# Edge rows in pairs of buffers, most of them summed by GpSimd, and a weight ring of three half chunks, in a one-core graph, attention and MLP layer

## The reference

```
xn    = layernorm(x)
e_f   = relu([xn[src], xn[dst]] @ W_class + b_class)      # one row per edge
logit = e_f @ W_a + b_a
alpha = softmax of logit over the edges with one dst
z     = segment_sum(alpha * xn[src], dst)
g     = relu([xn, z] @ W_hn or W_on + b)                   # 128 h nodes, 384 o nodes
x1    = x + g + linear_attention(xn)
out   = x1 + mlp(layernorm(x1))
```

## Time and profile before

| | |
|---|---|
| median of 3 runs | 787.0 us (785.25 to 787.54) |
| profiled execution, its own time | 785.15 us |
| its span (first to last instruction) | 783.4 us |
| mean granted TensorE clock | 0.923 |
| PE busy | 660.7 us (84%) |
| DVE busy | 505.2 us (64%) |
| ACT busy | 209.5 us (27%) |
| POOL busy | 259.7 us (33%) |
| moved by DMA | 163.40 MB |

### The profile page before, as it was taken

The page is one execution under the profiler, slowest core; times in us unless marked ns, Lnnn a source line. Parts: engine busy times, 40 slices in busy tenths (PEclk is TensorE's granted clock), DMA queues, the critical chain, the costliest instruction groups (busy, mean ns, idle before and its releaser), DMA issues. The chain is left out here.

```text
span 783.4 us, 8227 instructions
## 1 busy us (share of the span) xinstructions
PE 660.7 (84%) x2739; PEld 467.8 (60%) x2741; DVE 505.2 (64%) x1084; ACT 209.5 (27%) x266; POOL 259.7 (33%) x191
## 2 busy tenths in 40 slices
PE   4999999999847997798999699999955676798952
PEld 3778887788735775575778456677710011586621
DVE  8968813635645556365764597865568896327996
ACT  4333322220332354041614425152220100311001
POOL 3000306655654206247475555401223000002340
PEclk9999999999988999798999999999995779899985
DMA  9753449999999768969999999945360023140201
GB/s 347 257 203 135 141 184 298 296 323 320 323 303 317 269 200 226 306 200 312 306 287 296 317 318 236 303 151 189 108 242 0 0 80 135 54 140 5 108 27 80
DMA packets 41721, 163.40 MB, mean 209 GB/s; under 512 B 5168, under 2 KB 5552, under 8 KB 34512
## 3 DMA queue, kind: packets, MB, share of 16 engines
q0 software_dynamic: 20160, 73.41, 36.1%
q1 hardware_dynamic: 20800, 88.88, 30.1%
q10 hardware_dynamic: 720, 0.59, 0.2%
HBM read 146.08 MB, written 16.78 MB: 208 GB/s over the span
## 5 line engine op out<-in xcount | busy, mean ns | idle before, releaser
L1384 PE MATMUL bank_low<-w_hi,xT_hi 128*128 128x512 f32 x496 | 201.7, 407 | 8.2 <-DVE w_lo L861 3.2
L1385 PE MATMUL bank_low<-w_lo,xT_hi 128*128 128x512 f32 x496 | 196.4, 396 | 0.0
L1386 PE MATMUL bank_low<-w_hi,xT_lo 128*128 128x512 f32 x496 | 196.2, 396 | 0.0
L560 POOL DMA_INDIRECT gathered_rows<-edge_tables,dst_row x68 | 115.8, 1703 | 76.8 <-DMA gathered_rows<-edge_tables,src_row 65.5
L1029 DVE SCALAR_TENSOR_TENSOR gathered_rows<-gathered_rows,wa_bc 128x1024 f32<-128x1024 f32 x68 | 83.0, 1221 | 83.1 <-DMA gathered_rows<-edge_tables,dst_row 83.1
L560 POOL DMA_INDIRECT gathered_rows<-edge_tables,src_row x68 | 87.0, 1279 | 127.2 <-DVE gathered_rows L1029 91.8
L861 DVE TENSOR_TENSOR w_lo<-w_raw,w_hi 128x2048 fp32r<-128x2048 f32 x48 | 107.9, 2288 | 31.2 <-ACT w_hi L633 30.9
L1384 PEld LDWEIGHTS bank_low<-w_hi,xT_hi 128*128 128x128 f32 x496 | 95.3, 192 | 38.0 <-issue 12.3
L1386 PEld LDWEIGHTS bank_low<-w_hi,xT_lo 128*128 128x128 f32 x496 | 95.0, 191 | 20.6
L1385 PEld LDWEIGHTS bank_low<-w_lo,xT_hi 128*128 128x128 f32 x496 | 95.2, 192 | 18.7
L633 ACT ACTIVATE w_hi<-w_raw 128x2048 fp32r<-128x2048 f32 x50 | 92.8, 1902 | 8.3 <-DMA w_raw<-in_wt 8.3
(11 more groups left out here) (269 smaller groups left out, 951.7 us busy)
## 6 DMA issues: line engine op xcount, KB each, us to landing
w_raw<-in_wt SPq DMA_DIRECT2D x54, 1024.0 KB, 8.2
edge_tables<-stage SPq DMA_DIRECT2D x32, 256.0 KB, 7.1
x_in<-in_x SPq DMA_DIRECT2D x4, 512.0 KB, 9.1
xn_scratch<-xn SPq DMA_DIRECT2D x4, 512.0 KB, 4.6
node_top<-stage SPq DMA_DIRECT2D x8, 256.0 KB, 7.7
x_part<-in_x SPq DMA_DIRECT2D x8, 256.0 KB, 5.5
mix_out<-stage SPq DMA_DIRECT2D x8, 256.0 KB, 2.0
xn_raw<-xn_scratch SPq DMA_DIRECT2D x4, 512.0 KB, 5.8
```

What stands on the lines that cost most here:

```text
L560: pool.indirect_dma_start(rows_sum[:, s, :], None, table_d[0:rows, :], bass.IndirectOffsetOnAxis(ap=index[:, t:t + 1].bitcast(U32), axis=0 ...
L1384: pe.matmul(dest, lh, rh, start=start and i == 0, stop=False)
L1385: pe.matmul(dest, lh, rl, start=False, stop=False)
L1386: last = pe.matmul(dest, ll, rh, start=False, stop=last_one)
```

## The change

- **Buffers.** `SLOTS` goes from six single rows to five pairs: `rows[:, s, 0]` for src and `rows[:, s, 1]` for dst. `LAG` goes from 2 to 3 tiles.
- **Who sums.** Tiles with t % 3 == 2 (23 of 68) keep the DMA that adds. The other 45 gather both rows plainly, one after the other, and POOL sums them with a `tensor_tensor` of 128 x 1024 three tiles later.
- **Dots.** DVE takes single tiles (`edge_tile`), each with its mask, then the maximum of the tile before (`catch_up`), then its own dot. The table `TILES` gives for each chunk the tiles behind each of two points: after the low half 1 of chunk c, and after the low half 0 of chunk c + 1. Dots now go on up to PR0, and all 36 early lookups stand in PR1.
- **Weight ring.** The high and low parts lie in a ring of three half chunks (`w_half`) and not in two whole slots. PE goes through a chunk by halves: first k 0 to 3 of all row tiles, then k 4 to 7. High half 1 of chunk c + 1 can be made once the first halves of chunk c are multiplied (`first_halves`). SP loads half 1 of chunk c + 2 after the stores of chunk c.
- **Around the attention.** DVE's sums for K and Q follow all edge tiles of their chunk; `attend` and `invert_den` have new places; the products kv, den8 and attend on PE are placed by half.

```
-PAIRS = {4: 2, 5: 3, 6: 2, 7: 3, HHT0: 1, HHT1: 1, K0: 3, V0: 3, HN1: 1, K1: 3, V1: 3, Q0: 2, Q1: 3, ON0: 3, ON1: 1}
-MAXIMA = {PR0: (0, 18), PR1: (18, 36)}
+RING = 3
+TILES = {4: (0, 1), 5: (2, 3), 6: (2, 3), 7: (2, 3), HHT0: (1, 1), HHB0: (1, 1), HHT1: (1, 1), HHB1: (1, 1), K0: (3, 2), HN0: (0, 1),
+         V0: (3, 2), HN1: (0, 1), K1: (3, 2), V1: (3, 2), Q0: (3, 2), Q1: (2, 2), ON0: (2, 2), ON1: (2, 2), PR0: (3, 2)}
+MAXIMA = {PR1: (0, 36)}
-SLOTS = 6
+SLOTS = 5
+LAG = 3
+DMA_ADDS = [t for t in range(T_GATHERED) if t % 3 == 2]
+POOL_ADDS = [t for t in range(T_GATHERED) if t % 3 < 2]
...
+ATTEND = {(Q1, 1, 0): [(0, 0), (0, 1)], (Q1, 1, 1): [(0, 2), (0, 3)], (ON0, 1, 0): [(1, 0), (1, 1)], (ON0, 1, 2): [(1, 2), (1, 3)]}
+DEN8 = {(Q1, 0, 2): 0, (ON0, 0, 1): 1}
+KV_AT = {(HN1, 0, 0): 0, (Q0, 0, 0): 1}
...
@@ the loads, SP
+        def load_next(c, h):
+            sp.wait_ge(w_lo_done, 2 * (c - 1) + h + 1)
+            load_half(c, h)
...
@@ the gathers, POOL
             if t < T_GATHERED:
                 if t >= SLOTS:
                     pool.wait_ge(edge_dot, t + 1 - SLOTS)
-                gather(t, src_row, src_landed)
-            if t >= LAG:
-                u = t - LAG
+                gather(t, 0, src_row, src_landed)
+                if t not in DMA_ADDS:
+                    gather(t, 1, dst_row, dst_landed)
+            u = t - LAG
+            if u in DMA_ADDS:
                 pool.wait_ge(src_landed[u % SLOTS], 16 * (u // SLOTS + 1))
-                gather(u, dst_row, dst_added, ALU.add)
+                gather(u, 0, dst_row, dst_landed, ALU.add)
+            if u in POOL_ADDS:
+                s = u % SLOTS
+                pool.wait_ge(src_landed[s], 16 * (u // SLOTS + 1))
+                pool.wait_ge(dst_landed[s], 16 * (u // SLOTS + 1))
+                pool.tensor_tensor(rows[:, s, 0, :], rows[:, s, 0, :], rows[:, s, 1, :], ALU.add).then_inc(row_added, 1)
...
@@ the high halves, ACT
+            if h == 0:
+                act.wait_ge(prod_ready, FIRST[c - 1] + HEAD)
...
+            else:
+                act.wait_ge(first_halves, c)
...
@@ the order on DVE, tables
         for c in range(4, TABLES):
-            split_chunk(c + 1)
-            edge_work(c)
+            lo_half(c, 1)
+            edge_work(c, 0)
+            lo_half(c + 1, 0)
+            edge_work(c, 1)
```

More of the change, by code:

```diff
@@ L720, in _ @@
         for c in range(TABLES, BON0):
-            split_chunk(c + 1)
             if c == HHT0:
                 split_feat(1)
+            hi_half(c + 1, 0)
+            if c == K0:
+                copy_mlp_weights()
+            if c == K1:
+                copy_kv(0)
+            if c == Q0:
+                copy_kv(1)
+            if c != PR1:
+                hi_half(c + 1, 1)
+            if c == Q1:
+                for j in range(4):
+                    attend(0, j)
+            if c == ON0:
+                for j in range(4):
+                    attend(1, j)
             for i, m in enumerate(ROWS[c]):
@@ L1387, in split_product, with half_product @@
             return last
[L1389 to L1393 removed]
+        def half_product(b, c, h, m, lhs, start, stop, each_k=None):
+            hi, lo = w_half(c, h)
+            for k in range(4 * h, 4 * h + 4):
                 if each_k:
@@ L1403, in rows_product, with half_product_q @@
-            return last
+                cols = slice((k % 4) * CW, (k % 4 + 1) * CW)
+                pair = (lhs[0][k][:, m * P:(m + 1) * P], lhs[1][k][:, m * P:(m + 1) * P], hi[:, cols], lo[:, cols])
+                last = split_product(bank[b][:, :], [pair], start and k % 4 == 0, stop and k % 4 == 3)
+            return last
+        def half_product_q(b, c, h, i):
+            hi, lo = w_half(c, h)
+            pairs = []
+            for k in range(4 * h, 4 * h + 4):
+                cols = slice((k % 4) * CW + i * P, (k % 4) * CW + (i + 1) * P)
+                pairs.append((hi[:, cols], lo[:, cols], xT_hi[:, k, :], xT_lo[:, k, :]))
+            return split_product(bank[b][:, :], pairs, h == 0, h == 1)
@@ new lines, in add_bias, with first_chunk @@
+        def add_bias(b, c, start, stop):
+            return pe.matmul(bank[b][:, :], ones_b[:, :], b_hl[0:64, bias_no(c) % 2, :], start=start, stop=stop)
+        def first_chunk():
+            for m in range(MT):
+                pe.wait_ge(evac_done, m + 1)
+                for h in range(2):
+                    last = half_product(m, 0, h, m, xT, h == 0, False, lambda k: wait_first(m, k))
+                    if m == MT - 1 and h == 0:
+                        last.then_inc(first_halves, 1)
+                pe.wait_ge(bias_lo_done, 1)
+                add_bias(m, 0, False, True).then_inc(prod_ready, 1)
```

332 lines of the change are left out of this document (156 added, 176 removed).

## The result

| | before | after |
|---|---|---|
| median, us (4 runs each) | 786.2 (785.3 to 787.5) | 874.8 (874.3 to 879.1) |
| span of the profiled execution | 783.4 | 872.4 |
| PE, DVE, POOL busy, us | 660.7, 505.2, 259.7 | 692.5, 567.6, 362.6 |
| first, last dot starts, us | 132.4, 518.6 | 140.6, 613.7 |
| tail starts, us | 572.2 | 661.8 |

The ratio is 1.114, with an interval of 1.110 to 1.118: the change makes the kernel 11% slower. The forecast was 768 us, and the range ended at 799.

What follows compares the result with a forecast made beforehand. PE was held by waits that DVE ends, DVE by adding gathers, with DMA behind. Last dot 515 plus 38 us starts the tail at 553 instead of 572.2, so 787.0 - 19.2 = 768 us; likeliest 751 to 782, range ending at 799.

Steps and rivals of the forecast that it cites:

- the size of the loop: Adding gather, landing, dot, plain issues and POOL sum in sequence: 16.4 us per three tiles, or 5.5 per tile.
- the 5.7 taken from it: Forecast pace of edge tiles in us per tile, including 0.2 for POOL idling; 67 tiles put the last dot at 515.
- 7.0 + 0.8: In the gather loop: 7.0 us for the adding gather to land, 0.8 for DVE being amid a low half.
- With 10.9 it is 6.8: Gather loop with the median landing of 10.9 us instead of 7.0: 6.8 us per tile.
- 1.22 + 2.34 + 2.40 + 1.17 = 7.1: Rest of the gather loop: the dot, two plain issues, a POOL sum and one more issue.
- the bound behind the bound: The 16 DMA engines, share 1.02 in T4 to T7; 57 us less DMA time would make it 0.87.
- The rule against the change: POOL and DVE hold each other up at shared SBUF ports; counted at mean delays, 0.3 us per instruction.
- The end of PR1: Last dot to tail start: 38 us, with 12.5 before the lookups, 21.5 for them, then 2.3 and 1.7.
- The rival on the ring: Weight ring gives too little lead, costing PE 8 us in each of K0, K1, Q0, Q1: 792; chance 0.07.
- The slower rival: Gather loop is longer, 19 us per three tiles or 6.3 per tile: 808; chance 0.20.
- nothing gained: At 6.0 us per tile, PE's recovered waits go to lag and later lookups: 787; chance 0.07.
- my own forecast: Edge tiles at 5.45 to 5.9 us each, total time 751 to 782; chance 0.46.

Runs made afterwards that it cites:

- e12: Changed kernel with five single buffers, all tiles added by the DMA, no POOL sums, adding gather three steps behind: 868.4 us, ratio 1.103.
- e13: e12 with the adding gather two steps behind instead of three: 800.5 us, ratio 1.017.
- e9: Changed kernel with LAG = 2 and POOL's sums cut to 8 of the 1024 columns: 787.8 us, ratio 1.002.
- e7: e2 with destination rows gathered plainly over the source rows, so nothing is added: 757.0 us, ratio 0.961.
- e2: Changed kernel with ten single buffers, all tiles added by the DMA, no POOL sums, adding gather four steps behind: 777.9 us, ratio 0.990.
- e4: Changed kernel with all 68 tiles gathered plainly and summed by POOL, no adding gather: 884.1 us, ratio 1.121.
- e3: Changed kernel with POOL's sums cut to 8 of the 1024 columns: 840.4 us, ratio 1.069.
- e16: e10 with 11 small operations on POOL at the place of each sum: 840.8 us.
- e18: e10 with eight small operations on POOL at the place of each sum: 830.5 us.
- e1: Changed kernel with six single buffers, all tiles added by the DMA, no POOL sums, adding gather two steps behind: 783.7 us, ratio 0.998.
- e5: Changed kernel with LAG = 2, adding gather and sums both two steps behind: 839.0 us, ratio 1.066.
- e10: e5 with the 46 sums done by DVE instead of POOL: 795.3 us, ratio 1.011.
- e8: Changed kernel with only each fourth tile summed on POOL, the others added by the DMA, eight tiles in ten rows, three steps behind: 785.2 us, ratio 0.999.
- e6: Changed kernel with only the adding gather two steps behind, the sums still three behind: 841.3 us.
- e11: e2 with the all-reduce put behind PR0's four stage sums: 778.8 us, ratio 0.992.

## Why the prediction was wrong

**The step that failed** is the size of the loop: "16.4 us, or 5.5 per tile" and the 5.7 taken from it, where 7.06 was measured. The loop is there, with its members in their order. Over the 22 adding gathers (the trace has 46 sums, where the text before and the prediction count 45 and 23) the mean turn is 21.4 us (median 19.8). It falls in two parts:

- From the start of the adding issue to the dot: 10.1 us, against 7.0 + 0.8; 9.3 in the 17 cases where the dot waited for nothing else. The 6.7 of the earlier trace rows, counted from the same point, was one landing with a short issue (1.79 us), behind 4 us in which the DMA share was 0.33. The issue alone took 2.1 us in the mean and up to 3.64. Between 6.7 and the median of 10.9 I took the wrong end. "With 10.9 it is 6.8" stands in the prediction and comes near 7.06, but by luck: the landing was shorter than that and the other part longer.
- From the dot to the next adding issue: 11.2 us (median 9.8), against 1.22 + 2.34 + 2.40 + 1.17 = 7.1 and 1.5 for hold-ups. The two misses, 2.3 and 2.6 us, are of about one size. This part holds the other two tiles' work too: attention work, low halves and masks of DVE come between the dots of three tiles, and POOL waits in its queue for each of those dots (41 waits, 147 us). I had 0.2 us per tile for this.

The last dot came at 140.6 + 67 x 7.06 = 613.7 instead of 515. The first was late as well, 140.6 for the 133 reckoned with: POOL's first sum began at 138.2, after the 10.3 us of idle time that the experiments show to be no wait for rows. The prediction had nothing for it.

**What bounded it, and the lever that I missed.** e12 and e13 show that LAG against SLOTS decides: SLOTS - LAG tiles must cover issue, landing and dot of one adding gather. Before it was 6 - 2 = 4, and the change made it 5 - 3 = 2. I had both numbers in the loop's description, but never worked out what the loop would be with the old distance, which would have shown how much of it is choice. The distance alone is not the whole: in the changed kernel two steps behind instead of three give back 35.8 us, and it takes the sums' removal as well to give back the rest (e9).

**The DMA.** Its time fell by 42 us instead of 57, and its share to 0.80 as against 0.87: right in kind. That DMA was "the bound behind the bound" was right only in part: e7 takes 85 us from it and gets 21. The adding gathers' extra price, 1.26 us per tile, came out as 1.25 between e2 and e7. In the changed kernel it was 42 / 46 = 0.91, because plain gathers became dearer there: in e4, which has no adding gather, the queue takes 0.243 x 883.3 = 215 us for the packets that cost 195 in e7. Why is open.

**The rule against the change.** A maximum of 0.35 us took 3.16 beside a sum, and dots grew from 1221 to 1343 ns, maxima from 361 to 567, masks to 529. The Trainium skill ("SBUF — State Buffer", Who interferes with whom) has the pair of ports as an exclusive lock, and this case's trace agrees: a held instruction ends with the sum (204.29 and 204.14 us in the timelines above). DVE grew by 61 us of busy time (567.6 against 506.8 in e3). Yet in time the hold was the smaller part, by e16 and e18 at most about a quarter of what the sums cost on POOL rather than on DVE. I had it at "0.3 for each of eight instructions".

**The end of PR1.** From the last dot's start to the tail I had 38 us, it was 661.8 - 613.7 = 48.1. The chain of waits after:

```profile
613.69 1.25 DVE gathered_rows L1056 x2
615.63 3.85 POOL max_bc L602
619.77 6.72 issue
626.49 2.49 POOL stage L610 x2
628.99 2.01 DMA mix_out<-stage
631.58 1.91 ACT w_hi L658
658.67 2.20 DVE w_lo L885
```

12.5 us were to pass until the lookups, and they began 22.0 us behind the last dot's start, the high half that they wait for at 17.9. The reduce took 3.85 us in place of 1.8, and 6.7 us behind it nothing happened on POOL; before, the first stage sum waited for other data at that place, so the gap had no price and no row. ACT waited 26.8 us for a stage buffer meanwhile, and PE 9.5 us behind it, a wait that the prediction put at nothing and named as a sign against it. The lookups took 22.9 us (21.5 forecast).

**What held.** The tail: 872.4 - 661.8 = 210.6 us, 211.2 before. The rival on the ring is out by e1. The slower rival, given 0.20, was the right one in kind ("the adding gather still lands after some 9 us", each waits out the other), and it too was too small: 6.3 per tile and 808, against 7.06 and 875. The chances of 0.07 for nothing gained and 0.46 for my own forecast rested on a margin of 0.3 us per tile, with an uncertainty of over 1 us.

## What to carry to other kernels

Where one in-order queue both refills buffers and issues a second, dependent transfer, write down for that transfer which consumer it stands behind: buffers minus steps behind is the number of items that must cover issue, landing and use. Work that is moved to an engine whose queue feeds the pipeline costs as delay of the feed, however idle that engine looks on the page; here the same sums, counted from tile 2's dot on, cost 16 us on the busier engine and 47 on the other. And a loop that mixes waits in both directions is not the sum of its shortest rows: take each term at its mean under contention, or price the forecast by how far that mean may be off.

## What the runs showed of the hardware

- An adding gather costs the 16 DMA engines 1.25 us more than a plain one for a tile of 0.524 MB (e2, e7).
- POOL sat idle for 10.0 to 10.3 us between its last gather issue and its first tensor operation, of 8 or of 1024 columns, with the rows there already (after, e3, e5, e9; e10 dates the landing). In e8 and e6 it was 8.4 and 11.6 us.
- POOL sat idle for 7.9 us ahead of the all-reduce when a tensor operation came before it (e11), and for 6.7 to 7.2 us behind it ahead of the next one (after, e2, e11), with no other reason shown.
- The issue of an adding gather, 1.54 us at the least, took up to 3.64 us beside a low half of 2.28 us, longer than that half itself: it ended 1.4 us behind the half's end (after).
- 128x1024 f32 sums take 1.22 us on DVE and 2.47 to 2.51 on POOL; small ones of 8 columns 0.37 to 0.39 in a row.
